# Attention over 16 heads: q and k turned by VectorE's block transposes and a move through DRAM in place of TensorE, with another order of row tiles

## What is computed

```python
xn = _layernorm(x)
q, k, v = xn @ Wq, xn @ Wk, xn @ Wv            # 16 heads of 128
q, k = rmsnorm(q, q_rms_w), rmsnorm(k, k_rms_w)
scores = q k^T / sqrt(128) - slope[h] * distance   # causal
y = rmsnorm(softmax(scores) @ v, subln_w)
x = x + y @ Wproj + fp8_round(xn) @ w.T
```

## Time and profile before

| | |
|---|---|
| median of 3 runs | 547.68 us (547.47 to 548.8) |
| profiled execution | 549.33 us |
| its span | 547.2 us, mean granted TensorE clock 0.99 |
| TensorE busy | 521.6 us (95%) |
| VectorE busy | 417.8 us (76%) |
| ScalarE busy | 391.6 us (72%) |
| GpSimd busy | 333.9 us (61%) |
| DMA | 10.81 MB, mean 20 GB/s |

### The profile page before, as it was taken

One profiled execution on the slowest core, in us unless ns is written; L12 is line 12 of the kernel. 1 busy time (PEld: TensorE's weight loads), 2 busy tenths in 40 slices (PEclk: granted clock), 3 DMA queues, 4 the chain that ended last, 5 costly groups with the idle time before them and its releaser, 6 DMA issues.

```text
span 547.2 us, 11863 instructions
## 1 busy us (share of the span) xinstructions
PE 521.6 (95%) x3420; PEld 481.4 (88%) x3420; DVE 417.8 (76%) x1031; ACT 391.6 (72%) x887; POOL 333.9 (61%) x430
## 2 busy tenths in 40 slices
PE   6678999999999999999999999999999999999985
PEld 2667899999999999999999999999999999999874
DVE  5876768777787867878787777878678787868775
ACT  2367878686876968677696868768686877868662
POOL 3385587574758737676576748587376856747221
PEclk9699999999999999999999999999999999999999
DMA  5200100101010010101001010100101000000002
GB/s 158 58 2 1 40 1 1 40 2 40 2 38 0 0 38 0 38 0 38 0 1 37 0 38 0 38 0 9 30 0 38 0 10 0 10 2 1 2 1 77
DMA packets 18581, 10.81 MB, mean 20 GB/s; under 512 B 2176, under 2 KB 18560, under 8 KB 18560
## 3 DMA queue, kind: packets, MB, share of 16 engines
q1 hardware_dynamic: 17568, 10.49, 6.6%
q10 hardware_dynamic: 992, 0.07, 0.1%
HBM read 9.51 MB, written 1.05 MB: 19 GB/s over the span
## 4 chain that ended last, share of the span: by engine, by line
PE 86%; DVE 5%; ACT 4%; issue 2%; DMA 1%; POOL 1%; POOLq 0%; DVEq 0%; SPq 0%
PE pT_ps L562 11%; PE qkv_ps L477 10%; PE qkv_ps L479 8%; PE qkv_ps L478 8%; PE yT_ps L479 7%; PE yT_ps L478 7%; PE yT_ps L477 7%; PE score_big L477 5%; PE score_big L478 4%; PE score_big L479 4%; PE misc L538 3%; PE score_small L479 2%; PE score_small L478 2%; PE score_small L477 2%; ACT stage L734 1%
## 5 line engine op out<-in xcount | busy, mean ns | idle before, releaser
L919 DVE TENSOR_TENSOR pT_lo<-pT_ps,pT_hi 128x384 fp32r<-128x384 f32 (+1 forms) x192 | 101.0, 554 | 41.9 <-ACT pT_hi L762 41.2
L734 ACT ACTIVATE stage<-qkv_ps 128x384 f32<-128x384 f32 x119 | 58.5, 492 | 83.0 <-PE qkv_ps L479 82.3
L754 ACT ACTIVATE probs<-probs,neg_max 128x1024 f32<-128x1024 f32 (+7 forms) x128 | 98.4, 770 | 16.8 <-DVE neg_max L910 16.7
L762 ACT ACTIVATE pT_hi<-pT_ps 128x384 fp32r<-128x384 f32 (+1 forms) x192 | 86.2, 484 | 17.4 <-PE pT_ps L562 12.6
L431 POOL TENSOR_TENSOR y_r<-y_ms,minus_half 128x4 f32<-128x4 f32 x32 | 32.7, 1022 | 105.8 <-DVE y_ms L938 105.8
L477 PE MATMUL qkv_ps<-w_hi,xT_hi 128*128 128x384 f32 x242 | 87.9, 363 | 2.6 <-ACT stage L734 0.6
L562 PE MATMUL pT_ps<-ident,probs 128*128 128x128 f32 x576 | 84.5, 274 | 4.2 <-ACT probs L754 3.5
L478 PE MATMUL qkv_ps<-w_lo,xT_hi 128*128 128x384 f32 x242 | 82.0, 339 | 0.0
L479 PE MATMUL qkv_ps<-w_hi,xT_lo 128*128 128x384 f32 x242 | 81.9, 338 | 0.0
L391 POOL TENSOR_TENSOR qk_r<-qk_ms,minus_half 128x4 f32<-128x4 f32 x64 | 64.8, 1013 | 27.2 <-DVE qk_ms L884 25.6
L562 PEld LDWEIGHTS pT_ps<-ident,probs 128*128 128x128 f32 x576 | 66.3, 141 | 9.2 <-ACT probs L754 4.4
(11 more groups left out here) (183 smaller groups left out, 1313.3 us busy)
## 6 DMA issues: line engine op xcount, KB each, us to landing
w_raw<-in_wq SPq DMA_DIRECT2D x16, 128.0 KB, 2.2
w_raw<-in_wk SPq DMA_DIRECT2D x16, 128.0 KB, 2.3
w_raw<-in_wv SPq DMA_DIRECT2D x16, 128.0 KB, 2.3
wp_raw<-in_wproj SPq DMA_DIRECT2D x16, 128.0 KB, 2.1
acc<-in_x SPq DMA_DIRECT2D x2, 512.0 KB, 5.5
out<-acc SPq DMA_DIRECT2D x8, 128.0 KB, 1.8
w<-in_ffn_w ACTq DMA_DIRECT2D x1, 64.0 KB, 6.8
q_col<-in_q_w ACTq DMA_DIRECT2D x1, 0.5 KB, 2.9
```

Of the source, the lines that this page charges most:

```text
L734: act.activation(stage_of(h, k // 2)[:, k % 2, :], qkv_bank(h, k)[:, 0:3 * D], ACT.Copy).then_inc(qkv_read, 1)
L754: act.activation(probs[:, s % 2, 0:(i + 1) * P], probs[:, s % 2, 0:(i + 1) * P], ACT.Exp, bias=neg_max[:, par, s:s + 1], scale=-1.0, accum ...
L762: act.activation(pT_hi[g][:, a:b, r * P:(r + 1) * P], pT_ps[(CHUNK0[s] + k) % 2][:, 0:(b - a) * P].rearrange("p (j t) -> p j t", t=P), ACT ...
L919: dve.tensor_tensor(pT_lo[g][:, a:b, r * P:(r + 1) * P], pT_ps[(CHUNK0[s] + k) % 2][:, 0:(b - a) * P].rearrange("p (j t) -> p j t", t=P), ...
```

## The change

Three things change together.

First, q and k of heads 1 to 15 aren't transposed by TensorE. `turn_blocks` on VectorE transposes the 32x32 blocks of `qk_n` into `turned`; SP stores `turned` to a DRAM buffer `passed` and loads it back with the blocks in their places, in four DMAs of 32 partitions each, to `qk_raw`; `qk_hi` and `qk_lo` read that from SBUF. Head 0 still uses TensorE (`transpose_first`).

Second, `ORDER` is 3, 4, 2, 5, 1, 6, 0, 7. The first score needs the first two k only, and `NEEDS` tells how many each score waits for. `project(h + 2, 0)` is issued at the end of head h, and the projections of head h + 1 are moved forward by a place or so.

Third, the prologue is written anew: x comes in four DMAs, `dist` is built before the norm on GpSimd, `split_w(1)` waits for the normalised x, head 0 is projected as soon as half of x is there, ten filler matmuls stand before it, and the decoding of w8 is spread over the eight steps of head 0.

```diff
-    ORDER = [7, 0, 6, 1, 5, 2, 4, 3]
+    ORDER = [3, 4, 2, 5, 1, 6, 0, 7]
+    NEEDS = [max(ORDER[:s + 1]) // 2 + 1 for s in range(NT)]
...
+            def move_qk(h, k):
+                m = NPAIR * (h - 1) + k
+                sp.wait_ge(blocks_turned, m + 1)
+                past(sp, qk_moved[k % 2], 64 * (2 * (h - 1) + k // 2))
+                sp.dma_start(passed[k % 2], turned[:, k % 2, :]).then_inc(qk_put, 16)
+                sp.wait_ge(qk_put, 16 * (m + 1))
+                sp.wait_ge(qk_split, m + NPAIR - 1)
...
+                for b in range(4):
+                    sp.dma_start(qk_raw[32 * b:32 * b + 32, k % 2, :].rearrange("i (a r) -> i a r", a=4),
+                                 passed[k % 2].rearrange("(a i) (b r) -> b i a r", a=4, b=4)[b]).then_inc(qk_moved[k % 2], 16)
...
-            def transpose_qk(h, par, k, now):
-                bank_free(now, f"qkT{k}")
-                pe.wait_ge(qk_normed, NPAIR * h + k + 1)
...
+                if s == 0 or NEEDS[s] > NEEDS[s - 1]:
+                    pe.wait_ge(qk_split, NPAIR * h + NEEDS[s])
...
+            def turn_blocks(h, k):
+                m = NPAIR * (h - 1) + k
+                dve.wait_ge(qk_normed, m + NPAIR + 1)
+                past(dve, qk_put, 16 * (m - 1))
+                dve.transpose(turned[:, k % 2, :].rearrange("p (b n c) -> p b n c", b=4, n=4),
+                              qk_n[:, k % 2].rearrange("p t a (b c) -> p b (t a) c", b=4)).then_inc(blocks_turned, 1)
...
             def qk_lo(h, par, k):
-                dve.scalar_tensor_tensor(qT_lo[:, par, at], ps[:, 0:2 * P], q_col[:, 2:3],
-                                         qT_hi[:, par, at].bitcast(f32), ALU.mult, ALU.subtract)
-                dve.tensor_tensor(kT_lo[:, par, at], ps[:, 2 * P:4 * P], kT_hi[:, par, at].bitcast(f32),
-                                  ALU.subtract).then_inc(misc_read, 1)
+                for t in range(2):
+                    dve.scalar_tensor_tensor(by_block(qT_lo[:, par, at])[:, t], moved(k, 0)[:, t], q_col[:, 2:3],
+                                             by_block(qT_hi[:, par, at].bitcast(f32))[:, t], ALU.mult, ALU.subtract)
+                dve.tensor_tensor(by_block(kT_lo[:, par, at]), moved(k, 1), by_block(kT_hi[:, par, at].bitcast(f32)),
+                                  ALU.subtract).then_inc(qk_split, 1)
```

More of the change, by code:

```diff
@@ L39, in build_block @@
     CPH = CHUNK0[NT]
[L44 to L66, removed]
+    WIDE = 4
+    NEEDS = [max(ORDER[:s + 1]) // 2 + 1 for s in range(NT)]
     def past(eng, sem, count):
@@ L102, in build_block @@
         qk_n = sb("qk_n", [P, 2, 2, 2, D])
+        turned = sb("turned", [P, 2, 4 * P])
+        qk_raw = sb("qk_raw", [P, 2, 4 * P])
+        passed = [nc.dram_tensor(f"passed{b}", (P, 4 * P), f32, kind="Internal").ap() for b in range(2)]
         qT_hi = sb("qT_hi", [P, 2, T], f32r)
@@ L462, in head @@
                 split_wp(h, par)
+                if not last:
+                    norm_qk(h + 1, 3)
+                    split_v(h + 1, 1 - par, 3)
                 if after is not None:
@@ L656, in ffn @@
                 last.then_inc(ffn_ready, 1)
+            pe.wait_ge(const_ready, 2)
+            warm(WARM_UP)
+            transpose_x(0)
+            transpose_x(1)
+            warm(KEEP_WARM)
+            for k in range(NT):
+                if k % 4 == 0:
+                    pe.wait_ge(xT_read, KT * (k // 4 + 1))
+                if k == NT - 1:
+                    transpose_first(0)
+                project(0, 0, k)
+                if k == 1:
+                    transpose_x(2)
+                    transpose_x(3)
+            transpose_first(1)
+            project(1, 1, 0)
+            score(0, 0, 0)
+            transpose_first(2)
+            project(1, 1, 1)
+            transpose_first(3)
             def head(h, par, tile, after):
-                first, last = isinstance(h, int) and h == 0, is_last(h)
+                first, last = is_first(h), is_last(h)
                 for s in range(NT):
-                    if s == 2 and not last and not first:
-                        project(h + 1, 1 - par, 2)
+                    if s == 2 and not last:
+                        project(h + 1, 1 - par, 3)
                     if s < NT - 1:
@@ L668, in head @@
                     if s == 0:
-                        if not last and not first:
-                            project(h + 1, 1 - par, 0)
                         if not first:
                             attend(h - 1, 1 - par, 1, 0)
-                            turn_y(h - 1, 0, h)
-                    if s == 1:
                         if not last and not first:
@@ new lines, in head @@
+                    if s == 2:
+                        probs_hi(h, 1)
+                        if not first:
+                            y_out(h - 1, 1)
+                        exps(h, par, 2)
+                        if not last:
+                            copy_qkv(h + 1, 3)
+                            square_qk(h + 1, 1)
+                    if s == 3:
+                        if not last:
+                            copy_qkv(h + 1, 4)
+                        exps(h, par, 3)
+                        probs_hi(h, 2)
+                        if not last:
+                            copy_qkv(h + 1, 5)
+                            square_qk(h + 1, 2)
```

640 lines of the change are left out of this document (368 added, 272 removed).

## The result

The changed kernel takes **659.64 us** (median of 4 runs, 657.49 to 660.17) against 547.92 (547.47 to 548.8) for the kernel before on the same chip: 1.203 times as long, interval 1.200 to 1.206. The forecast was 534.5 us, with 516 to 553 as its range. The profiled execution took 660.03 us with a span of 657.9.

A forecast was written before the change was run, and what follows sets the result against it. TensorE was taken to bound the kernel, at 31.75 us per middle head. 547.2 - 7.0 (prologue) - 7.7 (14 middle heads) + 1.5 (tail) = 534.0 us of span, plus 0.5 gives 534.5 us; range 516 to 553.

The forecast's parts named there:

- Is 2.65 us of slack enough?: Middle head, VectorE's queue walked beside TensorE's: 3.3 us idle, so VectorE alone gives 30.7 us per head.
- Rival A: Middle heads: TensorE stays the bound and VectorE's idle gaps close up, 517.6 us; chance 0.25.
- TensorE's 30.0 us: TensorE's floor for a middle head: 31.75 us less 1.76 us for the transposes of qk_n it loses.
- What VectorE gains in work: VectorE per head: four block turns add 2.4 us, qk_lo about unchanged, 27.35 us of work in all.
- The port: VectorE's two-SBUF-input qk_lo instructions meet GpSimd: 0.5 us per head not absorbed, bounds 0 and 2.5.
- Rival B: Middle heads slower through the shared port: 33.2 us per head, total 562, or 551 to 562 partly absorbed; chance 0.2.
- the tail: End of the kernel, tile 7 last in place of tile 3: +1.5 us, bounds 0 to 2.5.
- The move through DRAM: Store and four loads per k: a chain of 5.7 us, costing nothing by itself until it exceeds 7 us.
- Prologue: Start through head 1's second score: first score near 27.5 us, second score of head 1 near 59, -7.0 us.

The follow-up runs named there:

- Experiment 1: Changed kernel with add_out(h-1, 0, 1) moved first in step 4 of VectorE's queue: 603.54 us.
- experiment 2: Changed kernel with twelve filler matmuls put in front of turn_y(h-1, 1) on TensorE, order unchanged: 633.11 us.
- experiments 7 and 10: 7: changed kernel, add_out(0,1) first and third pair's split earlier, 597.56 us; 10: that with qk_lo's two-input operations replaced and turns left out, 565.88 us.
- the ring cut: Changed kernel with add_out(0,1) first and third pair's split earlier, 597.56 us; with qk_lo's two-input operations also replaced for heads 2 to 15, 588.41 us.
- experiment 3: Changed kernel with qk_lo's operations of two SBUF inputs replaced by one-input block turns for heads 2 to 15: 637.89 us.

## Why the prediction was wrong

**The step that failed is "Is 2.65 us of slack enough?".** It walked VectorE's queue and wrote that "from 14 us on VectorE has an unbroken queue to the end of the head", with 3.3 us idle in all. For TensorE the text looks at the scores, one projection and the transposes of tile 7. It left out turn_y(h-1, 1), which waits until proj_added is 4(h-1)+2, that is for add_out(h-1, 0, 1), behind a block turn and three entries in VectorE's queue. The score of row tile 7 stands behind turn_y, and the mask behind that. VectorE was idle for 9.0 us of the 38.5 in place of 3.3. Experiment 1 shows it by moving that one entry: 56 of the 112 us.

**Its consequence for the clock** was nowhere in the prediction, which speaks of the clock only in the prologue. After the wait TensorE's matmuls run at the lower level; experiment 2 prices that at 26.5 us. Rival A and the forecast both took TensorE's 30.0 us as given.

**"What VectorE gains in work"** had the turns right (0.707 us each against 0.68, four per head) and the sum too small: 29.47 us busy per head instead of 27.35. Most of the difference is qk_lo, which was taken as unchanged: 4 x (2 x 0.456 + 0.553) = 5.9 us per head, against 4 x (0.48 + 0.42) = 3.6 by the earlier trace rows. That load is the second cause: with the two places put right, the turns and the two-input operations still cost 31.7 us (experiments 7 and 10).

**"The port"** was under-sized. 0.5 us per head was taken; replacing the operations gave 1.55 in the changed kernel and 0.65 with the ring cut, where up to 0.6 can be the shorter replacements, and the durations give 1.5, all within the bounds 0 to 2.5. Rival B had the right sign, but by its own price it ended at 562. The port was at most a fifth of the loss and not the mechanism.

**The new order** was priced at nothing beyond the tail and a 0.7 us overlap at tile 7. On the kernel before, the order alone costs 19.8 us.

**"The move through DRAM"** held: 256 KB stored in 2.0 us, 64 KB loaded in 2.0, and leaving it out gained nothing in two kernels.

**"Prologue"** was right up to the point where the loop begins. TensorE's timeline of the changed kernel, the first scores of heads 0 and 1 and the second of head 1:
```profile
27.79 0.50 PE L513 MATMUL score_small<-kT_hi,qT_hi 128*128 128x512 f32 x1 [1.40 <-DVE kT_lo L982]
...
61.29 0.47 PE L513 MATMUL score_small<-kT_hi,qT_hi 128*128 128x512 f32 x1
...
67.41 0.44 PE L513 MATMUL score_big<-kT_hi,qT_hi 128*128 128x384 f32 x1 [1.55 <-DVE kT_lo L992]
```
The first score was forecast at 27.5 and came at 27.79; the second score of head 1 was forecast at 59 and came at 67.41. Head 0 took 33.5 us instead of 31, and from the first to the second score of head 1 it was 6.1 us more, behind the transposes of tile 7 and a wait for kT_lo. Head 0 has no `add_out` and no turn_y, so this part of the loss isn't the wait for `add_out`; which entries make it, no run shows. On the kernel before, the prologue is worth 2.2 us by the medians, where 7.0 was forecast (1.05 of it for a projection done earlier, and with a first score that needs less of q and k than the old order's).

**What stays open.** Some 18 us of the 112, and beyond them the 13 us that were forecast as a gain: no run has the changed kernel's queues with the old order. Why the new order costs 20 us on the old queues was read from TensorE's waits and not tried; which entries would have to move with it isn't known. Of the first leg, the 2.5 us in front of mean_squares, released by ScalarE's squares, was forecast at 1.9 to 2.5 and stayed in every variant of the changed kernel (33 to 45 us over the run); no run takes it away.

## What to carry to other kernels

- When work moves from a full engine to one with slack, write down for every instruction of the engine that becomes free which semaphore it waits for and where in the other queue the release stands. A PSUM bank that is used again counts as such a wait. One release behind three entries that it does not need cost 56 us here, more than all the work that was moved.
- A wait on an in-order engine is priced by what stands behind it. 35 us of waits in the list were 56 us of time; 47 us of ScalarE's waits for DMA could be taken away and the time stayed, since the engines then waited for something else.
- Price a reordering by itself, on the old kernel: it is a change of one line, and here it was a loss of 20 us that nobody would have seen in the combined result.

## What the runs showed of the hardware

- An idle time of 2.8 us on TensorE lowered the granted clock for the matmuls behind it to the level of 1.2 GHz: steps of 0.42 us per 512 columns against 0.23. The same followed the wait of 2.04 us at 340.71, and didn't follow the one of 1.49 us at 302.20. Twelve matmuls that compute nothing, put into the wait of 2.8 us, took 26.5 us off the run.
- A VectorE operation with two SBUF inputs and a GpSimd operation that reads SBUF lengthened one another, and the one that started later was the long one. kT_lo at 312.64 began inside GpSimd's v_lo (312.46) and took 0.96 us in place of 0.41; the other way round, v_lo began at 325.10 inside a kT_lo that kept its 0.41, and took 0.92:
```profile
312.46 0.86 POOL L439 TENSOR_TENSOR v_lo<-stage,v_hi 128x256 fp32r<-128x256 f32 x1
...
325.10 0.92 POOL L439 TENSOR_TENSOR v_lo<-stage,v_hi 128x256 fp32r<-128x256 f32 x1
```
The Trainium skill (SBUF — State Buffer, Who interferes with whom) says that a VectorE instruction with two SBUF inputs contends with a GpSimd instruction that reads SBUF, and that the order of issue decides which of them blocks; the trace agrees. v_lo's shortest is 0.72, and beside a block turn, which has one input, it kept 0.72 to 0.75 in all 30 cases. Over the run the two operations of qk_lo were on average 48% and 35% longer than their shortest (experiment 3).
- A block turn of a 128x512 fp32 tile takes 0.707 us on VectorE, about the same as a subtraction of that size (pT_lo, 0.68).
